# Reordering the steps of a mixer, attention and router block on one core: SiLU behind its taps, later turned tiles, early copies of the attention outputs, stacked rows by four heads, and the next norm in a wait

## The reference

```python
x = L0_attn_hidden_states                       # (4, 512, 256), float32
x = x + mixer(layernorm(x), W_in, conv_w, ...)  # Mamba2: 32 heads of 64, state 128, 4 taps
x = x + ffn(layernorm(x), w1, w2, w3)           # ternary weights, hidden 704
x = x + attention(layernorm(x), W_qkv, W_o)     # 16 heads of 16, causal, with ALiBi
x = x + experts(layernorm(x), gate_w, ...)      # 64 experts, 6 per token, and a shared one
...
hBC = _silu(conv(xc, conv_w) + conv_b)          # mixer: every channel by itself, 4 taps
h = dA_t * h + u;  y = einsum('bhpn,bhn->bhp', h, C_t)
g = (y + D_param * xs) * _silu(gate)
...
attn = softmax(q @ k.T / sqrt(16) + alibi + causal)
y = attn @ v
```

## Time and profile before

| what | value |
|---|---|
| median of 3 runs | 1536.63 us (1531.63 to 1536.78) |
| the profiled execution | 1536.63 us, its span 1534.8 us |
| busy: PE, DVE, ACT, POOL | 1199.7, 909.1, 648.4, 584.1 us |
| mean granted TensorE clock | 0.902 of full speed |
| a row's stages, row 2: mixer | 735 to 882 us |
| small network, norm, q, k and v | 882 to 948 us |
| attention, then `between` | 948 to 1021 us, to 1073 us |
| experts and the last sums | 1417 to 1535 us |

### The profile page before, as it was taken

How to read it: one execution, slowest core, us unless ns; L and a number is a source line. 1 busy time by engine, 2 the same in 40 slices (tenths; PEclk the granted TensorE clock), 3 DMA queues, 4 the chain that set the end, 5 groups by cost and what they waited for, 6 DMA issues and landing times.

```text
span 1534.8 us, 23644 instructions
## 1 busy us (share of the span) xinstructions
PE 1199.7 (78%) x8164; PEld 731.2 (48%) x8166; DVE 909.1 (59%) x1766; ACT 648.4 (42%) x1496; POOL 584.1 (38%) x789
## 2 busy tenths in 40 slices
PE   3799977778999876878999867779899775779950
PEld 2355544454555543555555534455555533555520
DVE  4577764446877744446977653456877643453426
ACT  3644423556444232546444224546544123431540
POOL 2255531210477712210577621110677611116660
PEclk9899988899999987998999987998999876989985
DMA  7455543400333235200333247001333529028779
GB/s 280 148 182 183 179 112 40 47 2 19 111 110 111 88 79 60 25 2 32 127 108 105 67 79 81 4 9 36 118 108 110 169 65 137 16 82 300 151 105 372
DMA packets 105957, 159.50 MB, mean 104 GB/s; under 512 B 10816, under 2 KB 67776, under 8 KB 105152
## 3 DMA queue, kind: packets, MB, share of 16 engines
q1 hardware_dynamic: 91056, 129.63, 33.1%
q0 software_dynamic: 9216, 19.98, 5.1%
q10 hardware_dynamic: 5568, 8.39, 1.5%
HBM read 104.55 MB, written 40.83 MB: 95 GB/s over the span
## 4 chain that ended last, share of the span: by engine, by line
PE 54%; DVE 14%; issue 9%; POOL 9%; ACT 6%; DMA 5%; ACTq 1%; SPq 1%; POOLq 0%; DVEq 0%
PE bank L1057 12%; PE bank L1099 5%; PE bank L982 5%; DMA joint<-pool_b 3%; PE bank L1163 3%; PE bank L1086 3%; PE bank L1078 3%; PE bank L1242 3%; DVE nmax L1668 2%; PE bank L1093 2%; DVE pool_c L1516 2%; PE bank L1184 2%; PE bank L1227 2%; DVE joint L1532 2%; PE bank L1315 2%
## 5 line engine op out<-in xcount | busy, mean ns | idle before, releaser
L1057 PE MATMUL bank<-xnT,joint 128*128 128x512 f32 x544 | 268.8, 618 | 3.4 <-ACT joint L745 1.7
L1959 POOL TENSOR_TENSOR joint<-joint 128x512 f32<-128x512 f32 x128 | 168.5, 1318 | 238.8 <-DVE joint L1532 237.6
L1516 DVE SCALAR_TENSOR_TENSOR pool_c<-bank,params,pool_c 128x511 f32<-128x511 f32 (+2 forms) x216 | 161.1, 747 | 81.1 <-ACT pool_c L706 75.7
L1668 DVE TENSOR_REDUCE nmax<-bank 128x1 f32<-128x512 f32 (+3 forms) x176 | 108.6, 638 | 112.3 <-PE bank L1204 111.2
L1057 PEld LDWEIGHTS bank<-xnT,joint 128*128 128x128 f32 x544 | 99.8, 197 | 101.8 <-issue 93.0
L982 PE MATMUL bank<-consts,pool_c 128*128 128x128 f32 (+1 forms) x368 | 69.5, 291 | 82.3 <-ACT pool_c L715 39.9
L848 ACT ACTIVATE pool_c<-bank 128x512 f32<-128x512 f32 (+1 forms) x176 | 95.0, 553 | 89.7 <-PE bank L1229 89.4
L1099 PE MATMUL bank<-wout,pool_c 128*128 128x256 f32 x512 | 127.0, 393 | 1.2 <-DVE pool_c L1557 1.2
L745 ACT ACTIVATE joint<-bank,dt_ 128x64 f32<-128x64 f32 x512 | 111.6, 338 | 13.0 <-PE bank L982 12.9
L1099 PEld LDWEIGHTS bank<-wout,pool_c 128*128 128x128 f32 x512 | 99.1, 197 | 34.3 <-issue 21.7
L731 ACT ACTIVATE pool_c<-bank 128x512 f32<-128x512 f32 x64 | 38.2, 598 | 175.6 <-PE bank L1057 175.6
(11 more groups left out here) (266 smaller groups left out, 2415.3 us busy)
## 6 DMA issues: line engine op xcount, KB each, us to landing
pool_b<-dA_rows SPq DMA_DIRECT2D x64, 256.0 KB
pool_b<-dec_rows SPq DMA_DIRECT2D x96, 128.0 KB
joint<-pool_b SPq DMA_DIRECT2D x48, 256.0 KB, 13.8
acc<-xrow SPq DMA_DIRECT2D x13, 640.0 KB, 5.3
joint<-dA_rows SPq DMA_DIRECT2D x32, 256.0 KB
dA_late<-dA_rows SPq DMA_DIRECT2D x32, 256.0 KB
xslot<-xrow SPq DMA_DIRECT2D x16, 321.0 KB, 4.5
pool_b<-xslot SPq DMA_DIRECT2D x64, 80.2 KB, 2.6
```

Source lines behind the costliest of these rows:

```text
L1057: last = mm(bank[:, :], win[:, k, col:col + P], xnT[:, k, :], start=(k == 0), stop=(k == KD - 1))
L1516: ins = v.scalar_tensor_tensor(out=cv[:, n:L], in0=bank[:, 0:L - n], scalar=convw[:, ci, TAPS - 1 - n:TAPS - n], in1=cv[:, n:L], op0=ALU.m ...
L1668: max_done.inc(v.tensor_reduce(nmax[:, t * AH + h0:t * AH + h0 + nh], src, AX.X, ALU.max, negate=True))
L1959: M_ready.inc(p.tensor_tensor(M[u % 2][:, hs_, :], Lx[:, hs_, :], cbm[:, c * P:(c + 1) * P].unsqueeze(1).to_broadcast([P, 4, P]), ALU.mult))
```

## The change

It has six parts. (1) `mixer_steps` on ACT does tap, SiLU and skip term of an x tile one behind the other; `mixer_steps` on PE does `turn_in` of a step's first tiles behind `within` and `from_state`. (2) POOL's scatters lie in steps 0 to 11. (3) ACT's copy of an attention output is a step of its own ("copy") directly behind "values"; the turn stays where it was, and the step "rows" stands in the middle of a group's turns. (4) The stacked rows come in 24 DMAs of four heads (128 KB) with one semaphore for each four heads, and `AGROUPS` takes all four tiles of the first four heads, then those of the second, then the others as before. For that PE projects every other column of `wq` and `wk`, and `head_of` names the heads. (5) For the coming row DVE does `norm(0)` ahead of `qkv`, and PE waits for `qk_rest` before its transposes; ACT's load of the table for Exp comes behind the norm's copies. (6) The constant rows are loaded by two DMAs, last in their list.

```diff
-AGROUPS = [(t, q) for half in range(2) for t in range(T) for q in range(half * 2, half * 2 + 2)]
+AGROUPS = [(t, q) for q in range(2) for t in range(T)] + [(t, q) for t in range(T) for q in (2, 3)]
...
+        def head_of(q, h):
+
+            return q % 2 * (AH // 2) + 2 * h + q // 2
...
-                if i == min(1, turns - 1) and 1 <= g <= len(AGROUPS):
+                if i == turns // 2 and 1 <= g <= len(AGROUPS):
                     attention_steps.append(("rows", g - 1))
...
-            attention_steps.insert(min(i + 5, len(attention_steps)), ("turn", g))
+            attention_steps.insert(i + 1, ("copy", g))
+            attention_steps.insert(min(i + 6, len(attention_steps)), ("turn", g))
...
-                    for i, (qp, kp) in enumerate(zip(QPARTS, KPARTS)):
-                        r0, kp = BROWS + i * AD, kp + 3
-                        stacked[half].inc(sp.dma_start(qks[r0:r0 + AD, half * 8:half * 8 + 8],
-                                                       parts[half][:, qp:kp + 1:kp - qp, :]))
+                    for q in (2 * half, 2 * half + 1):
+                        four = parts[half][q % 2 * (P // 2):(q % 2 + 1) * (P // 2)]
+                        for i, (qp, kp) in enumerate(zip(QPARTS, KPARTS)):
+                            r0, kp = BROWS + i * AD, kp + 3
+                            stacked[q].inc(sp.dma_start(qks[r0:r0 + AD, q * AQ:(q + 1) * AQ], four[:, qp:kp + 1:kp - qp, :]))
...
                         if tile[0] == "x":
                             tap(tile)
+                            silu(tile)
+                            skip_term(tile)
                         else:
                             gate(tile)
-                    for tile in early + late:
-                        if tile[0] == "x":
-                            silu(tile)
-                            skip_term(tile)
...
-                    for tile in first:
-                        turn_in(tile)
                     if s < UNITS:
                         within(s)
                         if s % T:
                             from_state(s)
+                    for tile in first:
+                        turn_in(tile)
...
-                qkv()
                 if coming is not None:
+                    dve.wait_ge(ln_T.sem, ln_T.upto(pair_count(r, 2, 1)))
                     row(coming)
                     dve.wait_ge(xnext_loaded.sem, xnext_loaded.upto(coming + 1))
                     norm(0)
                     row(r)
+                qkv()
...
-                    if done is not None and 1 <= s <= T * TOPK // 2:
+                    if done is not None and 0 <= s < T * TOPK // 2:
...
-                        for i in range(2 * s - 2, 2 * s):
+                        for i in range(2 * s, 2 * s + 2):
                             scatter(i // TOPK, i % TOPK)
```

31 lines of the change are left out of this document (16 added, 15 removed).

## The result

The changed kernel takes 1421.5 us, median of four runs (1418.6 to 1423.4), beside 1534.1 us of the kernel before on the same chip. The ratio is 0.926, with a 95% interval of 0.924 to 0.929: 7.4% faster. The forecast was 1456 us, with a range of 1434 to 1494 us. The direction was right and the gain, some 113 us in place of 81, too small by more than the range allowed.

A forecast was written before the change was run, and what follows sets the result against it. PE was taken as nearly the bound in mixer and attention, so only its idle time could be won. 28.4 + 10.4 + 13.2 + 29 = 81 us off 1536.6 gave 1456 us, range 1434 to 1494.

The forecast's parts named there:

- copy and rows in attention: Inside attention: PE's waits for ACT's copy and part of those for POOL's parts of the maxima go, 29 us.
- stacked rows: Before attention's first score: six DMAs of 128 KB land 7.1 us earlier a row, 28.4 us in all.
- order of the mixer: In the mixer: 1.4 us won a group, 4.2 a row, less 1.6 in a row's first group; 10.4 us in all.
- scatters: Mixer's last group: without step 12's scatters 4.43 us go in each of three rows, 13.2 us.
- The norm's move: Before the scores: nothing by itself, but without it the stacking's 7.1 us would be cut to 3.5 in three rows.
- The sum is 38.8; I take three quarters of it, 29 us: Attention: copy's 32.7 us plus 6.1 for the parts, cut because removed waits partly turn up elsewhere; bounds 0 and 45.
- rival (a): Attention gives nothing back: PE's idle time moves to DVE's maxima or the exponentials behind the copy; 1485 us, chance 0.20.
- Rival (c): Stacking DMAs: the pace is one DMA, not its bytes, with a new wait of 9 us a row; 1520 us, chance 0.05.
- Rival (b): The mixer gains nothing because DVE, with the late x1, sets the pace in every group; 1485 us, chance 0.08.
- Rival (e): Slower by TensorE's clock in attention, half speed instead of 0.88; 1585 us, chance 0.06.
- Rival (d): Whole kernel: nothing is seen, within 0.5%, each removed wait replaced by another of its size; 1536 us, chance 0.05.
- attention's full 45 us: Upper bound of the attention term (32.7 + 12.3), from which the forecast case's low end of 1438 us was given.

The follow-up runs named there:

- c4: Kernel before plus only the two moved attention steps, ACT's copy directly behind the values and the rows in the middle of the next group: 1467.0 us (0.955).
- a4: Changed kernel with its stacked rows sent as two times six DMAs of eight heads (256 KB) and two waits, new group order kept: 1441.2 us (0.939).
- b6: Changed kernel with the mixer's order of before: ACT's SiLUs behind all taps and gates, PE's turns at the step's head, scatters still early: 1436.2 us (0.936).
- b3: Changed kernel with the scatters back in steps 1 to 12 of the mixer in place of 0 to 11: 1432.6 us (0.933).
- a3: Changed kernel with both attention steps put back, late copy and early rows, new group order kept: 1494.8 us (0.973).
- b1: Changed kernel with the coming row's norm back behind DVE's splits and its other work for the heads' rows: 1429.6 us (0.932).
- f1: Changed kernel plus spare matmuls in PE's wait for the stacked rows and ACT's taps first in step 0 of each row's mixer: 1412.2 us (0.920).
- d1: Kernel before plus only ACT's copy directly behind the values: 1517.7 us (0.989).
- d2: Kernel before plus only the rows of maxima in the middle of the next group: 1501.1 us (0.979).
- e1: Changed kernel plus spare matmuls in PE's wait for the stacked rows, 40 ahead of the first score, 100 in the last row: 1414.3 us (0.922).
- b4: Changed kernel with ACT's taps of both x tiles ahead of the SiLUs in step 0 of a row's mixer: 1419.1 us (0.925).
- c1: Changed kernel with the attention groups in their old order, stacking by fours and moved steps kept: 1429.4 us (0.931).

## Why the prediction was right, and where it was wrong

By the experiments the whole divides like this, in us (`c4` adds its steps to the kernel before, the others undo theirs in changed):

| part | forecast | measured | by |
|---|---|---|---|
| copy and rows in attention | 29 | 67.7 | `c4` |
| stacked rows | 28.4 | 19.7 | `a4` |
| order of the mixer | 10.4 | 14.7 | `b6` |
| scatters | 13.2 | 11.1 | `b3` |
| sum | 81 | 113.2 | two kernels: 112.6 |

That the sum meets the difference of the two kernels so closely is partly luck: the same two steps of attention undone in changed (`a3`) cost 73 us, which would make it 119. The norm's move, 8 us by `b1`, and the order of the groups, 5 to 8 us, serve the stacked rows and are not added a second time. No run undoes the constant rows in two DMAs or the later table load. The strided weights cost nothing that can be seen: the projections of q and k took 9.43 us in row 2, where they took 9.56.

**The step that failed** is "The sum is 38.8; I take three quarters of it, 29 us", with its bound of 45. Three things were wrong with it.

The waits counted were too few. Counted were the copy's 32.7 us and half of 12.3 us for the parts. In `c4` the parts' wait fell from 17.9 to 7.8 us, and a third wait that was not counted went too: the scores' for DVE's maxima, 7.0 us in 16 waits. First this wait in the kernel before, then the parts' in `c4`:

```profile
PE bank L1203 <- DVE nmax L1668: 7.0, 16, 0.6
```

```profile
PE bank L1215 <- POOL mparts L2025: 7.8, 8, 1.4
```

Recorded idle time removed: 32.7 + 10.1 + 7.0 = 49.8 us, over the bound already.

A recorded wait seems to be less than what it costs. A lone matmul of 128 columns stands in the trace for 0.22 us, and the next can start 0.06 us behind its start; idle time counts only from the end of the 0.22. By that a wait costs some 0.16 us more than its row says, which is an estimate from these two rows of `f1`:

```profile
870.52 0.22 PE L1218 MATMUL bank<-maskb,identb 128*128 128x128 bf16 x1
870.58 0.22 PE L1217 MATMUL bank<-joint 108*128 108x128 bf16 x1
```

With 80 waits fewer that is 12.8 us for `c4`, 62.6 in all, of 67.7. The same sum gives 15.7 us for `d1` (9.9 us of idle time, 36 waits fewer) of 16.9 measured, and 28.0 for `d2` (22.4 us, 35 waits) of 33.5. All three come closer than by idle time alone, but no run isolates the 0.16 us, so this share is argued. The Trainium skill ("TensorE: Matmul & The Clock Gate", section "Single matmul latency") gives a lone matmul some 166 ns beyond its columns at full clock. The 0.22 - 0.06 us of the rows are the same number, but no independent check of it, because the ends of matmuls are modelled in the profile.

What is left, 5.1, 1.2 and 5.5 us, may be the clock. Before, it fell a second time inside attention in rows 2 and 3 (0.57 from 994 to 1002), and in `c4` it did not. By the mean clock of the profiled executions (0.902, 0.904, 0.903, 0.910) and their spans, the time at the lower level was 301 us before and 282, 294 and 269 us in `c4`, `d1` and `d2`: the smallest rest goes with the smallest change. `a3` shows more of it. Against changed it has 46 us more of recorded waits for copy, parts and maxima, in 62 waits more, which makes 56 us with the 0.16; the rest of its 73 us goes with some 50 us more at the lower level.

The factor. That "a wait that goes in such a ring partly turns up at the next engine" is true of the copy alone: 32.7 us removed gave 16.9. But the next engine in the ring was POOL with the parts, and the change gave it time in the same stroke. The factor belonged to one half of the change without the other. For the two together it was wrong to take one; rival (a) is refuted by `c4`. In changed the wait for the copy is gone, that for the parts is 8.8 us and that for the maxima 2.3 us.

Of the 9.1 us behind the last score 6.1 belong to this term too, by `c4`: the last groups' turns and parts drain there.

**The stacked rows** were right as far as the first score: 29.5 us against 28.4, DMAs 1.1 us apart, PE waiting 2.3 us in row 2. The `step_products` took 1.97 us and not 3.6, which had been read at the lower clock. Rival (c) is refuted by `a4`: the pace goes by bytes from 256 to 128 KB. The Trainium skill ("DMA: Bandwidth & Descriptors", section "Anatomy of one DMA") gives each DMA a fixed cost of about 2.0 us, fitted for GpSimd's queue. Taken as a pace of SyncE's queue it would bring rival (c), and the trace does not agree.

As time the stacked rows were worth 19.7 us. The 28.4 us put the whole of the earlier start into the time, and 9.2 us of it were lost again between first and last score (47.7 us on average in `a4`, 50.0 changed). By rows 0 to 3 the loss is 1.4, 0.1, 1.9 and 5.8 us. The lower clock at the stage's head does not explain it, since from the first score on it lasts 8 to 9 us a row in `a4` and 9 to 10 in changed. What changed has and `a4` has not are idle stretches of PE 18 to 21 us behind the first score: 0.96 us in row 0, 1.56 us for DVE's maxima in row 2 and 3.07 us in the last, where the clock is at its lower level for 6.8 us from there on:

```profile
1204.43 0.29 PE L1235 MATMUL bank<-maskTb,identb 128*128 128x128 bf16 x1 [3.07 <-issue]
```

The first and the last are of the kind seen in `e1`, each beside a DMA of the instruction queue that took 1.8 us with a median of 1.06 us. The stretches stand where the loss is, but what makes them is not shown. In `b4`, whose attention is the same, they fall in rows 2 and 3, so the 9.2 us are those of one execution of each kernel.

**The norm's move** was costed right: 3.8 us a row at the first score without it (3.6 forecast). In time that was 8 us.

**The mixer** came out step by step. A group took 38.9 us and now 37.5: 1.4 us. A row's first group takes 37.0 in place of 36.7 us in row 0: 0.3 us lost, where 1.4 - 1.6 = -0.2 was forecast. By the measured 1.4 the first group's own loss is 1.7 us for the 1.6 charged. The mixer's term of 10.4 us is 10.8 by row 0 (2.7 us a row) and 14.7 by `b6`. Rival (b) is refuted by both. PE before turn 0, x2, turn 1, x3 and turn 3, beside the earlier trace rows:

```profile
729.97 0.60 PE L990 MATMUL bank<-consts,pool_c 128*128 128x128 f32 x4
731.24 1.98 PE L1065 MATMUL bank<-xnT,joint 128*128 128x512 f32 x4 [0.67 <-DVE pool_c L1523]
...
739.05 0.66 PE L990 MATMUL bank<-consts,pool_c 128*128 128x128 f32 x4 [0.97 <-DVE pool_c L1523]
742.58 1.99 PE L1065 MATMUL bank<-xnT,joint 128*128 128x512 f32 x4 [0.33 <-ACT joint L755]
...
751.37 0.60 PE L990 MATMUL bank<-consts,pool_c 128*128 128x128 f32 x4
```

Turns 0 and 3 no longer wait; turn 1 waits 0.97 us for DVE's convolution where it waited 0.24, and x3 waits for the scaling, both as said. The wait before x2, 0.67 us for DVE, was not forecast and was not there before. With turn 1's it makes 1.64 us, near the 1.48 + 0.24 us that turn 1 alone was to bear. The loss in the first group, beside the earlier trace rows:

```profile
77.73 0.76 ACT L716 ACTIVATE pool_c<-bank,params 128x512 f32<-128x512 f32 x1
78.52 2.32 DVE L1523 SCALAR_TENSOR_TENSOR pool_c<-bank,params,pool_c 128x511 f32<-128x511 f32 x3 [1.52 <-ACT pool_c L716]
80.90 3.64 PE L1065 MATMUL bank<-xnT,joint 128*128 128x512 f32 x4 [2.24 <-DVE pool_c L1523]
```

DVE's idle time is 1.52 us, forecast 1.6, and PE pays for it with 2.24 us. The clock pays too: the four matmuls of x2 behind it take 3.64 us where they took 1.88, at a granted clock of 0.62 from 80.0 to 84.5 (before, at the same matmuls: 1.00). `b4` takes it out of the mixer.

**The scatters**: from the second to the fourth `within` of the last group, beside the earlier trace rows, 812.75 - 799.80 = 12.95 us in row 2, where it was 17.39:

```profile
799.80 1.09 PE L1086 MATMUL bank<-joint 128*64 128x128 f32 x16 [0.29 <-POOL joint L1967]
...
812.75 1.09 PE L1086 MATMUL bank<-joint 128*64 128x128 f32 x16 [1.26 <-POOL joint L1967]
```

Undone, it cost 11 us in place of 13.2.

**Rival (e)**, a clock at half speed through attention, did not come: 0.90 in row 2 after, 0.88 before. Rival (d), nothing seen, is out by the result.

One slip of the prediction does not change it: with attention's full 45 us its own terms give 1439.6 us and not 1438.

## What to carry to other kernels

When several waits of one ring go in the same change, add up all of them, the small ones too, and take no share off for what moves on until you have asked where it would move and whether the change relieves that place as well. A short wait on TensorE may cost more than its recorded idle time; here 0.16 us a wait brought the sum closer to the measured time in three kernels, but was not isolated. A start won is worth its microseconds only if the stage behind it runs as before: of 29.8 us at the first score 19.7 arrived, so look for new idle stretches and for the clock there. And a stage that began behind an idle stretch began at the lower clock here; spare matmuls in the wait won 7 us.

## What the runs showed of the hardware

In row 2 of changed, PE was busy for 5.6 of the 8 us ahead of 876, and from there 10 us followed at 0.51 of the full clock:

```profile
868.00:876.00 8.00, 5.58 (x37) 4.87 (x35) 2.51 (x5) 5.53 (x10) 0.00 (x0) 1.00 0.94 122
876.00:886.00 10.00, 8.39 (x51) 5.55 (x52) 4.86 (x10) 4.67 (x9) 1.64 (x9) 0.51 1.14 121
```

With spare matmuls in the idle time the clock stayed at 1.00 at that place in rows 0 to 2. At two places of each row this was worth some 7 us of the kernel's time each.

DMAs that restack rows of 64 or 128 partitions of SBUF onto 16 went at 2.4 us for each 256 KB and 1.07 us for each 128 KB, some 110 and 122 GB/s, with the DMA share at 1.1: a fixed cost of each DMA was not to be seen in their pace.

While such DMAs ran, PE stood still for 0.6 to 3.1 us without a wait that the profile shows (changed: rows 0 and 3; `e1`: all four rows), each time with a 16 KB DMA of the instruction queue just before or in it. The kernel before, `a4` and `c4`, with DMAs of 256 KB, show no such stretch over 0.5 us, but neither does `c1`, with 128 KB. The cause is open.
